# Evacuating the router's logits four tiles at a time, with eight weight pieces split beside it

## The reference

```python
logits = xt @ gate_w.T                 # xt: layer-normed tokens, 4096 x 256; gate_w: 8 x 256
scores = jax.nn.softmax(logits.astype(jnp.float32), axis=-1)
biased = scores + gate_bias
_, indices = jax.lax.top_k(biased, TOPK)          # TOPK = 2
...
for e in range(E):                                # E = 8, each expert 256 -> 512 -> 256
    y = y + _mlp(xt, w1[e], w2[e], w3[e]) * combine[:, e:e + 1]
z = _mlp(xt, sw1, sw2, sw3)                       # the shared expert
return (y + z).reshape(shape)
```

## Time and profile before

| | |
|---|---|
| median of 3 runs | 2100.45 us (2094.32 to 2104.28) |
| profiled execution | 2099.02 us |
| its span, first to last instruction | 2097.3 us |
| mean granted TensorE clock | 0.933 |
| router: first weight DMA issued to next stage's first instruction | 537.4 to 582.76 us |
| shared expert's last row of result | 763.8 us |

### The profile page before, as it was taken

How to read it: one execution, slowest core, us unless ns; L and a number is a source line. 1 busy time by engine, 2 the same in 40 slices (tenths; PEclk the granted TensorE clock), 3 DMA queues, 4 the chain that set the end, 5 groups by cost and what they waited for, 6 DMA issues and landing times. The chain is left out here.

```text
span 2097.3 us, 45658 instructions
## 1 busy us (share of the span) xinstructions
PE 1748.2 (83%) x14369; PEld 1164.1 (56%) x14375; DVE 1394.8 (67%) x2959; ACT 1113.3 (53%) x2609; POOL 979.6 (47%) x1528
## 2 busy tenths in 40 slices
PE   0588888887477879999996899999999999997467
PEld 0344445444334446666664677777777777775223
DVE  4356666766566634444444787888888888877796
ACT  1256666665543212222221666666666666676766
POOL 1655555550644112232223566666666666653004
PEclk9689999999589989999997999999999999999697
DMA  3000000000523011222223322222333233321002
GB/s 106 10 12 12 10 10 10 10 5 1 159 78 100 16 41 56 62 78 68 68 59 83 93 72 72 73 71 73 82 76 86 71 78 75 81 62 34 9 1 80
DMA packets 89635, 117.64 MB, mean 56 GB/s; under 512 B 16808, under 2 KB 59056, under 8 KB 89520
## 3 DMA queue, kind: packets, MB, share of 16 engines
q1 hardware_dynamic: 81072, 94.28, 16.7%
q0 software_dynamic: 6528, 17.83, 3.1%
q10 hardware_dynamic: 1920, 4.19, 0.6%
HBM read 56.36 MB, written 17.83 MB: 35 GB/s over the span
## 5 line engine op out<-in xcount | busy, mean ns | idle before, releaser
L1068 POOL TENSOR_SCALAR a_P<-a_P,a_RS 128x256 f32<-128x256 f32 x512 | 253.0, 494 | 229.7 <-DVE a_RS L1361 198.9
L1242 ACT ACTIVATE a_P<-a_pS,a_NM 128x256 f32<-128x256 f32 x512 | 238.0, 471 | 175.4 <-DVE a_NM L1357 174.0
L815 DVE TENSOR_REDUCE a_M<-a_pS 128x2 f32<-128x512 f32 x256 | 164.6, 685 | 144.0 <-PE a_pS L626 143.5
L1251 ACT ACTIVATE a_PH<-a_pT 128x512 f16<-128x512 f32 x256 | 153.5, 600 | 68.5 <-PE a_pT L1164 61.8
L1357 DVE TENSOR_REDUCE a_NM<-a_pS 128x2 f32<-128x512 f32 x256 | 174.6, 682 | 19.9 <-PE a_pS L1156 14.4
L1367 DVE TENSOR_TENSOR a_PL<-a_pT,a_PH 128x512 f16<-128x512 f32 x256 | 172.5, 674 | 12.0 <-ACT a_PH L1251 11.9
L754 ACT ACTIVATE a_PT<-a_pT 128x512 f32<-128x512 f32 x256 | 138.9, 597 | 71.3 <-PE a_pT L645 71.0
L1164 PE MATMUL a_pT<-g_ident,a_P 128*128 128x128 f32 x1024 | 155.3, 274 | 18.6 <-POOL a_P L1068 18.5
L1164 PEld LDWEIGHTS a_pT<-g_ident,a_P 128*128 128x128 f32 x1024 | 118.8, 141 | 39.2 <-POOL a_P L1068 24.6
L2017 ACT ACTIVATE me_hh<-me_pH 128x512 f16<-128x512 f32 x72 | 43.0, 597 | 175.2 <-PE me_pH L2004 155.7
L1155 PE MATMUL a_pS<-a_KD,a_QS 128*128 128x256 f16 x512 | 125.7, 273 | 0.0
(11 more groups left out here) (452 smaller groups left out, 5187.0 us busy)
## 6 DMA issues: line engine op xcount, KB each, us to landing
a_KD<-a_KN SPq DMA_DIRECT2D x128, 128.0 KB
a_QS<-a_QN SPq DMA_DIRECT2D x128, 128.0 KB
ms_stage<-mw SPq DMA_DIRECT2D x36, 256.0 KB, 2.7
ys<-me_yb SPq DMA_DIRECT2D x72, 128.0 KB
a_ctxin<-ctxT SPq DMA_DIRECT2D x32, 256.0 KB, 2.8
a_KZ<-a_KN SPq DMA_DIRECT2D x64, 128.0 KB
g_X<-x SPq DMA_DIRECT2D x1, 4096.0 KB
rows<-mr_row SPq DMA_DIRECT2D x32, 128.0 KB, 2.0
```

What stands on the lines that cost most here:

```text
L815: nc.vector.reduce_max(M[:, :, a, p2], pS[a][:], AX.X).then_inc(s_max.sem, 1)
L1068: last = nc.gpsimd.tensor_scalar(P32[u % 4][:, a, :], P32[u % 4][:, a, :], RS[u % 4][:, a:a + 1], LIFT, ALU.mult, ALU.mult)
L1242: last = nc.scalar.activation(P32[u % 4][:, a, :], pS[u % 2][:, a, :], ACT.Exp, bias=NM[u % 4][:, a:a + 1], accum_out=SM[u % 4][:, a:a + 1])
L1251: nc.scalar.activation(PH[p2 % 2][:, :, :, j * P:(j + 1) * P].rearrange("p a k q -> p (a k) q"), pT[u % 2][:].rearrange("p a k q -> p (a k ...
```

## The change

Four tiles' logits go next to one another into one bank of PSUM (`pL` has the form 128x4x8, with two such buffers in place of three of 128x8), PE signals once after the fourth, and ACT evacuates 128x32 numbers in one instruction. ACT does so in iterations 5, 9, ..., 29 and once behind the loop: 8 evacuations in place of 32. The number of jobs that are split beside the router goes from 9 to 8; the ninth, w2 of expert 1, goes to the head of the shared expert's list, which then has 38 half jobs in place of 36.

```diff
--- before.py
+++ after.py
@@ -1401,7 +1401,7 @@
 def moe_router(nc, ctx, X, mean, rstd, XT, gw_d, gb_d, gb, rows_d, L, consts, jobs):
 
     s = Scope(nc, ctx, "mr")
-    NS, NR, NL, PIECE = 4, 4, 3, F0 // 2
+    NS, NR, NL, LG, PIECE = 4, 4, 2, 4, F0 // 2
     xn = [s.sb(f"xn{i}", [P, D]) for i in range(2)]
     row = [s.sb(f"row{i}", [P, 2, D], F16) for i in range(NR)]
     nb = s.sb("nb", [P, TILES])
@@ -1409,7 +1409,7 @@
     gin = s.sb("gin", [P, KD, NE])
     gwh, gwl = s.sb("gwh", [P, KD, NE], F16), s.sb("gwl", [P, KD, NE], F16)
     pX = [s.ps(f"pX{i}", [P, 2, KD, P], F16) for i in range(2)]
-    pL = [s.ps(f"pL{i}", [P, NE]) for i in range(NL)]
+    pL = [s.ps(f"pL{i}", [P, LG, NE]) for i in range(NL)]
     xn_ready, hi_ready, lo_ready = s.counter("xn_ready", 1), s.counter("hi_ready", 1), s.counter("lo_ready", 1)
     xt_full, xt_ready, l_full, l_out = s.counter("xt_full", 1), s.counter("xt_ready", 1), s.counter("l_full", 1), s.counter("l_out", 1)
     stored = [s.counter(f"stored{i}", 16) for i in range(NR)]
@@ -1495,9 +1495,9 @@
                     xt_full.wait(act, t, 1 - NR)
                 nc.scalar.activation(row[t % NR][:, 0, :], xn[t % 2][:], ACT.Copy).then_inc(hi_ready.sem, 1)
 
-            def logits(t):
-                l_full.wait(act, t, 1)
-                nc.scalar.activation(L[:, t, :], pL[t % NL][:], ACT.Copy).then_inc(l_out.sem, 1)
+            def logits(n):
+                l_full.wait(act, n, 1)
+                nc.scalar.activation(L[:, n * LG:(n + 1) * LG, :], pL[n % NL][:], ACT.Copy).then_inc(l_out.sem, 1)
 
             act.wait_ge(nb_ready, 1)
             normalise(0)
@@ -1508,9 +1508,9 @@
                 if t + 2 < TILES:
                     normalise(t + 2)
                     high(t + 2)
-                if t:
-                    logits(t - 1)
-            logits(TILES - 1)
+                if t >= LG and t % LG == 1:
+                    logits(t // LG - 1)
+            logits(TILES // LG - 1)
 
         @block.tensor
         def _(pe):
@@ -1527,11 +1527,14 @@
 
             def logits(t):
                 xt_ready.wait(pe, t, 1)
-                if t >= NL:
-                    l_out.wait(pe, t, 1 - NL)
+                n, a = t // LG, t % LG
+                if n >= NL and a == 0:
+                    l_out.wait(pe, n, 1 - NL)
                 ts = slice(t * P, (t + 1) * P)
-                three_products(nc, pL[t % NL][:], lambda kt: XT[:, 0, kt, ts], lambda kt: XT[:, 1, kt, ts],
-                               lambda kt: gwh[:, kt, :], lambda kt: gwl[:, kt, :], KD).then_inc(l_full.sem, 1)
+                last = three_products(nc, pL[n % NL][:, a, :], lambda kt: XT[:, 0, kt, ts], lambda kt: XT[:, 1, kt, ts],
+                               lambda kt: gwh[:, kt, :], lambda kt: gwl[:, kt, :], KD)
+                if a == LG - 1:
+                    last.then_inc(l_full.sem, 1)
 
             transposes(0)
             for t in range(1, TILES):
@@ -2084,7 +2087,7 @@
     IDS = s.sb("IDS", [P, SLOT_TILES], U32)
     gb = s.sb("gb", [P, NE])
     flat = "p k n -> p (k n)"
-    NOW = 9
+    NOW = 8
     jobs = [(w_d[n][e].rearrange("(k p) n -> p k n", p=P), W[n][0][:, e, :, :].rearrange(flat), W[n][1][:, e, :, :].rearrange(flat))
             for e in (NE, *range(NE)) for n in ("w1", "w3", "w2")]
     with ExitStack() as c2:
```

## The result

| | before | after |
|---|---|---|
| median of 22 runs each | 2094.49 us (2088.06 to 2109.38) | 2087.57 us (2082.27 to 2101.46) |
| profiled execution, its span | 2099.02, 2097.3 us | 2083.67, 2082.0 us |
| mean granted TensorE clock | 0.933 | 0.939 |

The ratio is 0.9961 with a 95% interval of 0.9944 to 0.9977: 8.2 us less, between 4.8 and 11.7. The medians differ by 6.9 us. The other half is the effect itself: -6.9 or -8.2 us where -0.9 was forecast.

A forecast was written before the change was run, and what follows sets the result against it. POOL's ninth job was taken to end the router, 1.04 us behind the tiles' chain. Router -2.3 (1.04 + 0.64 + 0.6) and shared expert +1.4 gave -0.9 us: median 2100.45 to 2099.5, range 2093.5 to 2107.

The forecast's parts named there:

- The router: Router: without the ninth job, its load and 24 evacuations it ends 2.3 us earlier; bounds 0.7 and 4.3.
- this term: Router, tile 24: with the ninth job's load gone, ACT's 0.64 us wait for a store goes; bounds nothing and 0.64.
- The 0.6 us for 24 evacuations fewer: Router, ACT's tile chain: fewer evacuations save 0.6 us after DVE takes back a part; bounds nothing and 1.44.
- The price in steps 19 and 20: Shared expert: two more half jobs put POOL beside DVE's patterns and cost 1.4 us; bounds 0.5 and 1.8, or 2.6.
- Two of my terms: Shared expert: POOL slows step 19's last pattern by up to 0.47 us and two or three of step 20's by 0.8 to 1.31.
- ACT's share: Shared expert, step 20: ACT's 1.3 us for two more casts cost nothing, or 0.8 us if their cover were gone.
- The rival of a clock that falls in the products of step 20: Shared expert, 48 second-layer products: granted clock falls after PE's longer pause, costing 4.9 us, net +4.0, 2104.5 us; chance 0.12.
- their sizes are the same, so steps 1 to 18 stay as they are: Shared expert: all half jobs move by two places with unchanged sizes, so steps 1 to 18 change by nothing.
- the same elsewhere, to the good: Rival: an earlier stage start misses a low clock stretch, costing 2.5 us less, net -3.4, 2097.1 us; chance 0.07.
- the named cases: Whole kernel: forecast and rivals alone give 2097 to 2104.5 us, all within 0.5%, which has 0.94.

The follow-up runs named there:

- the kernels with copies: 3, 6 or 8 ACT copies behind the router's last evacuation in the changed kernel, 5, 7 or 12 in the kernel before; ratios 0.9955 to 1.0017.
- now8_only: The kernel before with eight jobs beside the router in place of nine, still an evacuation for every tile; ratio 0.9989 (0.9967 to 1.0011).
- group_only: The changed kernel with nine jobs beside the router again, so only the evacuation of four tiles at once; ratio 0.9984 (0.9965 to 1.0004).
- the first pair: The first profiles of the kernel before and the changed kernel; profiled executions 2099.02 and 2083.67 us.
- after_now7: The changed kernel with seven jobs beside the router and 40 half jobs in the shared expert; ratio 0.9987 (0.9965 to 1.0008).
- again_before: The kernel before, unchanged, measured and profiled again as a control; median 2094.38 us, ratio 0.999 (0.9968 to 1.0012).
- again_after: The changed kernel, unaltered, measured and profiled again; median 2088.07 us, ratio 0.9966 (0.9945 to 0.9986) to the kernel before.
- before_copies12: The kernel before with twelve ACT copies (into float16) behind the router's last evacuation; ratio 1.0017 (0.9996 to 1.0037).
- before_38: The kernel before with the last job split twice, giving 38 half jobs behind nine jobs in the router; ratio 0.9986 (0.9972 to 1.0).

## Why the prediction was right or wrong

Here are the means of the ten profiles with nine jobs in the router beside those of the eight with eight jobs there and 38 half jobs behind. The line of the router leaves out the kernels with copies and the two long routers told of at the end. Steps a to b are the time from the silu of step a to that of step b; steps 19 and 20 end with the silu of step 21.

| | nine jobs | eight jobs | difference | predicted |
|---|---|---|---|---|
| router | 44.2 us | 41.7 us | -2.5 | -2.3 |
| shared expert, steps 1 to 12 | 64.9 | 61.7 | -3.2 | 0 |
| steps 12 to 19 | 40.9 | 40.7 | -0.2 | 0 |
| steps 19 and 20 | 13.0 (36 half jobs) | 14.1 | +1.1 | +1.4 |
| last 48 products of the second layer | 6.6 | 5.6 | -1.0 | 0 |
| whole shared expert | 182.4 | 179.0 | -3.4 | +1.4 |

**The router was right**, -2.5 us for -2.3. POOL no longer ends it; the tiles do, with the last evacuation and the last store's landing at the same moment. Tile 24 starts 0.94 to 1.02 us behind its neighbour and waits for no store. But this term was not the ninth load's alone: `high(24)` waits 0.03 us in now8_only and as little in group_only, which keeps the load. An evacuation of 128x32 costs 0.20 us and 0.08 of cadence. The 0.6 us for 24 evacuations fewer is not confirmed either: now8_only has 42.2 us with all 32 evacuations, and the four grouped kernels with eight jobs and no copies have a mean of 41.5, but these four differ by 1.4 us among themselves (40.8 to 42.2).

**The price in steps 19 and 20 was right** in kind and nearly in size: +1.1 for +1.4 us. In the first pair it is 12.4 to 13.2 us, and the patterns of step 20 carry all of it (2.41 - 1.59 = 0.82 us, the same by which PE's wait grows). Two of my terms did not come up there: the last pattern of step 19 and the first of step 20 keep their 0.45 us. ACT's share is hidden. The rival of a clock that falls in the products of step 20 did not happen in the changed kernel: 690 to 694 us shows 1.00. It did with two half jobs more, in after_now7, and cost 1.7 us there where I had reckoned 4.9.

**The step that failed** is "their sizes are the same, so steps 1 to 18 stay as they are". Steps 1 to 12 became 3.2 us shorter, and three steps carry 2.9 of it. Step 6 takes 4.6 us where it took 6.0 in the means and step 10 5.0 for 5.9; both wait for a load. Step 4 takes 8.7 for 9.3, at a mean granted clock of 0.79 where it was 0.74. In step 6 ACT waits for the load of half job 11. Timeline of ACT and table of DMAs from the load's issue (618.2) to its landing in again_before:

```profile
622.58 0.63 ACT L1684 ACTIVATE mo_w2h<-ms_stage 128x512 f16<-128x512 f32 x1 [3.72 <-DMA ms_stage<-mw]
...
q8 instruction: 1, 0.02, 1.3%
...
ms_stage<-mw SPq DMA_DIRECT2D x2, 256.0 KB, 3.9
```

The same in again_after, issue at 620.9:

```profile
623.34 0.63 ACT L1687 ACTIVATE mo_w3h<-ms_stage 128x512 f16<-128x512 f32 x1 [1.81 <-DMA ms_stage<-mw]
...
q14 instruction: 1, 0.01, 0.9%
...
ms_stage<-mw SPq DMA_DIRECT2D x2, 256.0 KB, 2.5
```

The load of 256 KB takes 622.58 - 618.23 = 4.35 us in the first and 623.34 - 620.89 = 2.45 in the second. In the first, a transfer of the queue that fetches the program's own instructions lies within it. The transfer that the second table shows is one of 8 KB; the bar of the same answer has it 0.5 us after the issue, ahead of the load's own packets:

```profile
DMA  0000000300000033993745699798964000000000
```

This load takes 4.1 to 4.6 us in 7 of the 10 profiles with nine jobs in the router and 3.1 in one more, with a fetch that starts 1.0 to 2.6 us after the load's issue, and 2.4 to 2.8 in all 10 with eight or seven. A later load, that of half job 19, takes 3.2 to 3.7 us in 9 of the 10 with nine jobs and in 2 of the other 10; step 10 takes 5.8 us or more in just these eleven and 5.0 or less in the rest.

That the slow loads come from the fetches is read from the traces; no run moved a fetch alone. But the traces say it clearly. From half job 3 on, none of the 579 loads of the twenty profiles that overlap no fetch takes more than 2.96 us. Of the 105 that overlap one, 41 take 3.02 to 4.61 us. The moment matters: all nineteen loads with a fetch of 16 KB that starts 0.6 to 1.7 us after their issue take 3.05 us or more, while half job 11 in now8_only meets one 2.2 us after its issue and takes 2.73.

Where the fetches fall goes with what the router executes, and for the one at half job 11 not with the ninth job. A fetch of 16 KB starts 40.1 to 42.1 us into the stage in all ten profiles with 32 evacuations, now8_only among them, and 46.3 to 52.3 us in all ten with 8, group_only among them. Tables of DMAs for this load, in now8_only from 626.1 and in group_only from 615.95 us to its landing:

```profile
q8 instruction: 1, 0.02, 2.1%
...
q14 instruction: 1, 0.01, 1.1%
```

| router | profiles | load of half job 11 | step 4 | step 6 | step 10 | steps 1 to 12 |
|---|---|---|---|---|---|---|
| nine jobs, 32 evacuations | 9 | 2.9 to 4.6 us | 9.2 us | 6.1 us | 5.8 us | 65.0 us |
| nine jobs, 8 evacuations (group_only) | 1 | 2.8 | 9.9 | 4.8 | 6.2 | 63.9 |
| eight jobs, 32 evacuations (now8_only) | 1 | 2.7 | 8.6 | 4.8 | 4.8 | 61.5 |
| eight jobs, 8 evacuations | 7 | 2.4 to 2.8 | 8.8 | 4.6 | 5.0 | 61.8 |

So step 6 is short with either half of the change; steps 4 and 10 are short only with eight jobs, as far as one profile of each half tells. Why the load of half job 19 and the clock in step 4 go with the eight jobs stays open.

The last 48 products take 7.0 to 7.1 us where the granted clock is 0.50 for 3.4 us of it, and 5.4 at 1.00 throughout. Windows over the stage's end, again_before and again_after:

```profile
752.50:760.00 7.50, 6.04 (x41) 4.78 (x41) 1.91 (x5) 0.63 (x1) 0.00 (x0) 0.77 0.00 0
```

```profile
753.00:760.00 7.00, 5.05 (x47) 4.53 (x48) 2.65 (x5) 0.63 (x1) 0.00 (x0) 1.00 0.02 4
```

A low stretch began 173.9 to 177.3 us into the stage in those profiles, just where the products stand. It comes in seven of the eight profiles with 36 half jobs behind the long router, in one of the ten with 38 half jobs (behind either router), in the one with 40, and not in the one with 36 behind the short router. The rival "the same elsewhere, to the good" named this mechanism and had a chance of 0.07; it worked out 2.5 us for the low stretch of step 4. That stretch was not missed: between 16 and 31 us into the stage the clock is at 0.50 for 10.2 us in both profiles of the first pair, at 16.9 to 20.3 and 23.7 to 30.5 us before and at 17.6 to 27.8 after. It lies elsewhere, and step 4 is shorter by 1.3 us there and by 0.6 in the means. So it was the right sort of event and too small, and it did not contain the loads.

**From stages to the whole.** -2.5 - 3.4 = -5.9 us lies in the two stages, of the 6.9 between the medians and the 8.2 of the ratio. A further part is in the upper tail: the kernel before, in all its runs here, took more than 2100 us in 49 of 183; the variants of it that keep nine jobs and single evacuations in 16 of 96; the changed one and its variants with eight or seven jobs in 3 of 116; now8_only and group_only, with half of the change each, in 1 of 12 each. Without such runs the means of the first comparison are 2092.6 and 2087.7 us, 4.9 apart. Both profiles that show a wait of 12.6 us, the last section's, are of the tail (2106.66 and 2103.22 us) and no other profile is above 2100. That the tail is made of that wait is argued from these two, and why the change makes it rarer stays open.

**The measure of the unseen** was wrong as well: the named cases were all of single events, each within 5 us, on an execution whose untouched stages vary by 15 us, and three runs gave me a base 6 us too high.

## What to carry to other kernels

Cut two profiles into stages before explaining a difference, and profile each kernel a second time: here the largest difference of the first pair, 6.5 us, was in a stage that nobody had touched and changed sign in the next pair. A step that keeps its work can still change with the moment at which its loads go out, so "the sizes are the same" is no reason to cost a stage at zero when it is bound by loads that are waited for; leave room for it in the range, and look in the table of DMAs for fetches of the program's own instructions beside the slow ones. When a change has two parts, see that the other experiments do not carry both: here only two profiles of twenty part them. And take work off an engine only until the next chain ends the stage: going from nine jobs to eight shortened the router by 2.5 us, from eight to seven by 1.5 in one profile, and the second step cost 2.8 us in steps 19 and 20 of the stage that took the work over, 1.7 of it by the clock.

## What the runs showed of the hardware

**A DVE instruction that waited for 25 GpSimd instructions.** In two of twenty profiles the low half of tile 4, 0.46 to 1.01 us in the other eighteen, took 12.57 and 12.58 us. Timelines of DVE and of POOL in before_copies12 (its kernel lines stand one further down than in the one before):

```profile
542.28 12.57 DVE L1470 TENSOR_TENSOR mr_row<-mr_xn,mr_row 128x256 f16<-128x256 f32 x1 [6.00 <-ACT mr_row L1497]
...
542.88 1.42 POOL L1456 CAST mo_w2h<-mr_stage 128x256 f16<-128x256 f32 x4
544.27 2.54 POOL L1460 TENSOR_TENSOR mo_w2l<-mr_stage,mo_w2h 128x256 f16<-128x256 f32 x4
...
552.03 2.54 POOL L1460 TENSOR_TENSOR mo_w3l<-mr_stage,mo_w3h 128x256 f16<-128x256 f32 x4
562.09 1.62 POOL L1456 CAST mo_w2h<-mr_stage 128x256 f16<-128x256 f32 x4 [7.52 <-DMA mr_stage<-mw]
```

POOL's casts and subtractions follow one another without a gap and at their undisturbed pace (four casts in 1.42 us, four subtractions in 2.54), and DVE's instruction ends when POOL runs out of loaded weights, at 554.6. POOL then waits 7.5 us for the next load, since SP's loads stand behind stores that wait for this row. The router took 59.6 and 54.7 us in place of 44.2. The same in before_38, with the same instruction of DVE:

```profile
545.03 12.58 DVE L1469 TENSOR_TENSOR mr_row<-mr_xn,mr_row 128x256 f16<-128x256 f32 x1 [6.03 <-ACT mr_row L1496]
```

The Trainium skill (SBUF — State Buffer, section Who interferes with whom) has the second of the two wait for the whole of the first. Here it waited for some 25 in a row; the 1.01 us at most of the other eighteen fit the page's case. In all twenty profiles DVE comes back to this instruction from 3.7 to 6.0 us of idle time while POOL is at work without a gap; what makes it wait so long in two of them stays open.

**Loads that meet a fetch of the program's own instructions are often slower**: of the 256 KB loads in the twenty profiles, from half job 3 on, none of 579 without a fetch took over 2.96 us, and 41 of 105 with one took 3.02 to 4.61. A change in one stage moves the fetches of the next: with 24 evacuations fewer in the router one of them went from 40.1 to 42.1 us into the shared expert to 46.3 to 52.3.

**An untouched stage of PE work varies by 15 us** (478 to 494) between executions of the same instructions, in the pair shown with the share of its time at half clock: PE busy 388.76 us at a mean of 0.94 and 398.19 at 0.92 for the same 3808 products. Over the twenty the mean clock tells only a part: the stage took 479.6 us at 0.91 in one profile and 482.8 at 0.96 in another.
